# Edge stream: GpSimd waits in the middle of each chunk's gathers for TensorE's last pair of picks

## What is computed

```python
h = (x_flat @ W_gat).reshape(M, HEADS, NUM_EXPERTS)        # M = 16384
src = jnp.concatenate([edge_index[0], loops])              # 262144 edges + 16384 loops
dst = jnp.concatenate([edge_index[1], loops])
e = jax.nn.leaky_relu(a_src[src] + a_dst[dst], negative_slope=0.2)
ee = jnp.exp(e - jax.ops.segment_max(e, dst, num_segments=M)[dst])
denom = jax.ops.segment_sum(ee, dst, num_segments=M)
msg = h[src] * (ee / (denom[dst] + 1e-16))[:, :, None]
agg = jax.ops.segment_sum(msg, dst, num_segments=M)
```

## Time and profile before

| what | value |
|---|---|
| median of 3 runs | 5086.44 us (5078.35 to 5090.78) |
| span of the profiled execution | 5093.1 us |
| span less the runs' median | 6.7 us |
| mean granted clock of TensorE | 0.738 of full speed |
| busy: TensorE, VectorE, ScalarE, GpSimd | 60%, 55%, 46%, 44% of the span |
| gathers of the edge stream | 1632, from 830.4 to 4504.1 us |
| picks of the edge stream | 13056 matmuls |
| turns of VectorE in it (line 1049) | 68, the first at 917.2, the last at 4540.3 us |

### The profile page before, as it was taken

How to read it: one execution, slowest core, us unless ns; L and a number is a source line. 1 busy time by engine, 2 the same in 40 slices (tenths; PEclk the granted TensorE clock), 3 DMA queues, 4 the chain that set the end, 5 groups by cost and what they waited for, 6 DMA issues and landing times. The chain is left out here.

```text
span 5093.1 us, 63233 instructions
## 1 busy us (share of the span) xinstructions
PE 3045.9 (60%) x21149; PEld 2318.6 (46%) x21149; DVE 2806.7 (55%) x5784; ACT 2362.3 (46%) x4288; POOL 2224.4 (44%) x2218
## 2 busy tenths in 40 slices
PE   3656663666566566566566566566566566544775
PEld 2445542554454454455455455455455455432443
DVE  8857883445445445445445445445445445467986
ACT  3636655444444444444444444444434434404886
POOL 7865613334434434434434434434434434426530
PEclk7657775777777777777777777777777777766887
DMA  1111101111111111111111111111111111112101
GB/s 58 24 22 20 22 7 44 24 23 27 31 23 27 31 23 27 31 23 27 31 23 27 31 23 27 31 23 27 31 23 27 31 23 27 25 27 75 38 19 33
DMA packets 157528, 145.13 MB, mean 28 GB/s; under 512 B 71240, under 2 KB 133080, under 8 KB 156776
## 3 DMA queue, kind: packets, MB, share of 16 engines
q1 hardware_dynamic: 88656, 109.49, 6.4%
q0 software_dynamic: 68768, 34.45, 6.2%
HBM read 92.97 MB, written 50.82 MB: 28 GB/s over the span
## 5 line engine op out<-in xcount | busy, mean ns | idle before, releaser
L937 PE MATMUL es_pgot<-hash_space,es_pick 128*128 128x256 bf16 x13056 | 1835.9, 288 | 1423.7 <-issue 1418.8
L857 POOL DMA_INDIRECT es_got<-node_table,late x1632 | 1548.1, 949 | 2127.0 <-DVEq L1077 1649.7
L937 PEld LDWEIGHTS es_pgot<-hash_space,es_pick 128*128 128x128 bf16 x13056 | 1302.8, 101 | 1899.6 <-issue 1742.7
L1019 DVE TENSOR_TENSOR es_prod<-es_pgot,es_own 128x512 f32<-128x512 f32 x272 | 187.7, 690 | 1801.6 <-PE es_pgot L937 1627.7
L871 ACT ACTIVATE es_pick<-es_away,consts 128x512 bf16<-128x512 f32 x1088 | 680.0, 711 | 7.0 <-DMA es_away<-sorted_keys 6.6
L293 POOL DMA_INDIRECT fr_ring<-in_emb,fr_rows x384 | 456.0, 1188 | 209.8 <-issue 112.8
L875 ACT ACTIVATE es_pick<-es_pick,consts 128x4096 bf16<-128x4096 bf16 x136 | 503.6, 3703 | 0.9
L894 ACT ACTIVATE ex_hid<-ex_phid,weights 128x256 f32<-128x256 f32 x128 | 53.6, 470 | 692.7 <-PE ex_phid L944 692.3
L1039 DVE TENSOR_TENSOR es_hot<-es_iota,late 128x1024 bf16<-128x1024 f32 x272 | 331.7, 1219 | 33.4 <-DVE es_st L1079 25.7
L1040 DVE TENSOR_TENSOR es_hot<-es_iota,late 128x1024 bf16<-128x1024 f32 x272 | 330.2, 1214 | 0.0
L894 ACT ACT_TABLE_LOAD x32 | 41.1, 1283 | 559.2 <-PE ex_phid L944 559.2
(11 more groups left out here) (351 smaller groups left out, 4294.6 us busy)
## 6 DMA issues: line engine op xcount, KB each, us to landing
es_away<-sorted_keys SPq DMA_DIRECT2D x68, 512.0 KB
es_got<-node_table,late POOLq DMA_INDIRECT x1632
edge_states<-es_st SPq DMA_DIRECT2D x68, 384.0 KB
expert_outputs<-ex_y SPq DMA_DIRECT2D x64, 256.0 KB
bk_y<-expert_outputs SPq DMA_DIRECT2D x8, 2048.0 KB
fr_ring<-in_emb,fr_rows POOLq DMA_INDIRECT x384
out_dram<-h SPq DMA_DIRECT2D x4, 1024.0 KB, 5.1
late<-in_edges SPq DMA_DIRECT2D x1, 2048.0 KB, 9.3
```

Source lines behind the costliest of these rows:

```text
L857: pool.indirect_dma_start(out=got[:, r, k, :], out_offset=None, in_=table_dram, in_offset=bass.IndirectOffsetOnAxis(ap=src[:, n, k:k + 1]. ...
L937: mm = pe.matmul(p_got[:, q, c * 256:c * 256 + 256], pick[:, r, q // 2, k, at * P:at * P + P], parts[:, part, k], start=(k == 0 and part = ...
```

## The change

One wait is added to GpSimd's program. In every chunk n but the first, after 12 of its 24 gathers, GpSimd waits until `s_got_p` has reached 4n, which is when TensorE has finished pair 3 of chunk n-1. It then issues the other 12.

```diff
                 if n >= 2:
                     pool.wait_ge(s_free[r], n // 2)
                 for k in range(GC):
+                    if n and k == GC // 2:
+                        pool.wait_ge(s_got_p, n * PAIRS)
                     pool.indirect_dma_start(out=got[:, r, k, :], out_offset=None, in_=table_dram,
```

## The result

The changed kernel takes 4844.46 us (median of 4 runs, 4831 to 4854) against 5088.33 us of the kernel before: a ratio of 0.9524, 95% interval 0.9503 to 0.9545. It is faster, as forecast, but by 244 us and not by 136, outside the forecast range (4860 to 5180).

The account below looks back on a forecast made before the run. VectorE waits for TensorE, which crawls while gathers are issued. Turns of 52.5 us, not 54.6, give -134, the stage's start -14, the end +10: -138 on 5093.1, 4955, stated as 4950 us; range 4860 to 5180.

Parts of the forecast that it names:

- The lag of 6.0 us in both bursts: TensorE runs 6.0 us at full rate after each burst of gathers starts, on a stock of ready work, then crawls.
- B: Moved burst of twelve gathers behind pair 3, starting at T-3.6; its crawl lasts T+2.4 to T+15.15, 12.75 us.
- The slower rival: Stock still empty when B starts, so its crawl starts 1.6 us in: 56.7 us a turn, about 5216 us; chance 0.19.
- the stock lasts longer: Rival: 7.5 us of lag in both bursts, crawls 1.5 us shorter each, turn 49.7, 4770 us; chance 0.12.
- A: Burst of twelve gathers that stays, after the buffer is freed: starts T+25.1, crawls from T+31.0 to T+43.85.
- T: Start of one turn of the edge-stream loop; times such as T+20.9 count microseconds from it.
- The stage's start: GpSimd stops after 36 gathers, not 48, so the crawl under the four first pairs ends sooner: -14 us.
- The end: Last three turns: A and B join to one burst of 24; 42, 51 and 46 us against 128.9: +10 us.
- Only the number of gathers counts: No-change rival: crawls sum to what they were, turns within 0.2 us of 54.6, 5070 to 5100 us; chance 0.11.
- Theory A: Experiments: the crawl comes whenever gathers go on over 6 us, however spaced; one fill ahead of each gives ratio 1.055.
- Theory B: Experiments: each gather takes about 1.4 us of a service TensorE needs; gathers 1.44 us apart give ratio 0.79 to 0.90.
- B2: Experiments: the service goes by the gather as such, so half-row gathers crawl as before, ratio 0.96 to 1.02.

Follow-up runs that it names:

- e9: Changed kernel with its wait ahead of the first of the 24 gathers, not the thirteenth; with the crawl 0.9967 of the kernel before, 54.6 us a turn.
- e8: Changed kernel with portions of 8 gathers and two waits instead of one; with the crawl 0.9380 of the kernel before, 50.1 us a turn.
- e15: Changed kernel, unedited, run again against the kernel before, without the crawl: 3396.13 us, ratio 0.9999.
- e7: Kernel before with one GpSimd fill of a scratch tile ahead of every gather, no wait in the middle; with the crawl 4293.67 us, ratio 0.8456.
- e17: Kernel before with one scratch fill ahead of each gather and the wait in the middle; with the crawl 4202.80 us, ratio 0.8230.
- e18: Kernel before with gathers of 64 rows instead of 128 from the third chunk on; with the crawl ratio 1.0179.
- e10: Kernel before with every gather of the edge stream reading the same 128 table rows; with the crawl ratio 0.9995.
- e16: Kernel before with gathers of 64 rows instead of 128 from the third chunk on; without the crawl ratio 0.983.

## Why the forecast was wrong, point by point

*What bounds the kernel: right, in the sets with the crawl.* VectorE waited for TensorE and TensorE for something that goes with the gathers.

*The lag of 6.0 us in both bursts: right as a number, open as a mechanism.* It is 5.8 us (median of the bursts of 12) in the changed kernel, also in B, which starts about 5.3 us after a crawl's end (1484.77 to 1490.08). The slower rival (0.19) fails here: its crawl would have started 1.6 us into B. Whether a stock of ready work is what lasts 5.8 us was only argued. Signals of TensorE that are late while it still runs at full rate fit a rival as well: something behind TensorE fills up and does not hold it until it is full. No run separates the two. At the stage's start fourteen gathers and not twelve had been issued when the first picks began (830.35 to 846.58), which fits either.

*The length of a crawl: wrong, and this is the step that failed.* The prediction took over "the full rate returns 5.0 us after the last gather" from bursts of 24 and charged 12.75 us to a burst of 12. The tail is not a constant, it is the backlog of the burst, 3.2 us after 12: the crawls were 11.4 and 11.0 us. The kernel before had the two lengths that show it: 5.0 us after 24 gathers and 8.2 us after the 48 at the stage's start, 889.00 to 897.20; only the first was used. The measured 4844 us lies in the range of the rival "the stock lasts longer" (4740 to 4890), and its crawls, 1.5 us shorter than forecast, came true; but they were shorter at their end, with a lag of 5.8 and not 7.5 us, so its number fits by luck. A constant tail also makes the second way of the sum (52.7 us) too high, and I raised 52.2 to 52.5 for its sake.

*What a crawl lets through: too much for B, and the clock too cheap.* 19 matmuls in a crawl held for A (19) and not for B: its 12 in 11.35 us are fewer than the 15 in 11.0 us of the earlier trace rows, which the prediction had named as a sign against it. And the 47 matmuls behind B took 7.67 us at a granted clock of 0.66, where 5.7 us for 43 were charged. So the 1.3 us by which B's crawl ended sooner (T+13.9, not T+15.15) were given back: pair 1 was done at T+21.5 against a forecast of T+20.9, A began at T+25.8 and not T+25.1. VectorE's new waiting in the first half came as foretold: 10.5 us in two waits, 4.68 us for pair 0 and 5.80 for pair 1. The first of them is a late signal, which the prediction did not have: by its sum the last matmuls of pair 0 are the first thing done in the crawl. In the second half VectorE waits 9.31 and 3.18 us, 12.5 where some 15 were forecast.

*The sum of a turn: order of events right, size off.* The gain is 3.5 us a turn where 2.1 were forecast: 51.1 us and not 52.5. Over 64 turns that is 89 us of the 106 by which the forecast missed the median. Not all of the 1.4 us is the crawls. Medians over the turns put the take of the last pair at T+47.8, where 48.6 was forecast. The two crawls together are about 3 us shorter than charged, but a later start of A's crawl (0.5 us), fewer matmuls inside B's and slower ones behind both leave only some 0.5 us of it. Another 0.35 us is the step from pair 3's last matmul to the take, charged at 0.5 and measured at 0.15 (so it stood in the earlier trace rows too, 1568.84 to 1568.99). About 0.2 us is the step from the take to the next turn, which is 3.2 and 3.6 us by turns and not always 3.6, and 0.3 us is the raise to 52.5. That the wrong tail did not make the error larger is luck: the clock charged too low stood against it. The turn shown is one of the longest, 51.7 us with pair 3's end at T+48.0 (forecast T+48.1).

*The stage's start: right,* 16.0 us for 14. *The end: wrong sign,* 5.5 us gained for 10 lost; the three turns took 44.0, 43.4 and 36.0 us against 42, 51 and 46. The crawl of the joined burst was charged like a full one under the last two turns. I did not follow those turns in the trace.

*"Only the number of gathers counts" (0.11): refuted* by e9 and e8: 24 gathers a turn in bursts of 24, of 12, and of 8 and 16 give 54.6, 51.1 and 50.1 us.

*The rule that a DMA never contends with a compute engine* (the Trainium skill, "SBUF — State Buffer", "Who interferes with whom"): in three of seven sets nothing here speaks against it, and in the one of them in which the changed kernel ran (e15) its time was the same. In the other four it did not hold. The profile of the kernel before that the prediction used was of the second kind, and nothing in it says that there is a first.

*Theory A of the experiments* (any gathers longer than the stock make a crawl) fell with e7: 1.44 us apart, 0.846 and not 1.055. Theory B, that each gather takes some 1.40 us of a service that TensorE needs too, stands: e7, e17, e18 and the tails. The train of the first stage, 149 gathers in 217 us, fits it: 1.46 us apart on average. By B2 it goes by the gather, not by its rows (e18) or their places (e10). What the service is stays open. It is not the gathers' data: the DMA engines move 0 GB/s between 1564.50 and the crawl's end at 1567.40. And next to no instructions are read from memory meanwhile (12 packets in 3300 us). TensorE's signals are late together with its issue, so it may be their path; no run tests that.

## What to carry to other kernels

A stall that a burst leaves behind can be a backlog: read its tail at two lengths of burst before charging it, since a tail that grows with the count means that requests come faster than they are served, and then spacing them by little more than the missing time is worth far more than moving them (here 0.19 us a gather: 15%, the wait in the middle: 5%, both: 18%). Splitting a burst pays when the slowed engine stands the first microseconds of each part unharmed; moving it whole paid nothing here. Where an engine waits for one that is slowed, compare the signal's arrival with the end of the work it stands for: here 12 us lay between. Measure the kernel before on more than one occasion: a change that is worth 5% in one may be worth nothing in another, and a cure like the fills costs 10% there.

## What the runs showed of the hardware

The same program on the same kind of chip takes 3397 us or 5090 to 5120 us, and stays at one of them for a whole set of runs (up to 16 runs of the kernel before in a set, all within 0.6%). It is not the chip: e15 and e16 ran without the crawl and e17 and e18 with it, on the same chip, some time apart. That leaves what is decided when a program is loaded or when a set is set up; no run here tells which. The traces differ ahead of the edge stream too, though less: its first gather comes at 761 to 770 us without the crawl and at 811 to 833 us with it. Every run of the changed kernel and of the experiments is on record with a span and a granted clock, and the profiled execution of the changed kernel is one of the four timed (4831.48 us, span 4829.7). So "timed without a profile" does not hold for them, and whether there is a crawl when nothing is recorded is not shown.

In a deep crawl TensorE's matmuls are issued singly, in steps of about 0.7 us. In the changed kernel at the stage's start, TensorE in order of time:

```profile
851.33 0.37 PE L939 MATMUL es_pgot<-hash_space,es_pick 128*128 128x256 bf16 x1 [2.43 <-issue]
854.83 0.37 PE L939 MATMUL es_pgot<-hash_space,es_pick 128*128 128x256 bf16 x1 [3.12 <-issue]
857.63 0.37 PE L939 MATMUL es_pgot<-hash_space,es_pick 128*128 128x256 bf16 x1 [2.43 <-issue]
860.44 0.37 PE L939 MATMUL es_pgot<-hash_space,es_pick 128*128 128x256 bf16 x1 [2.44 <-issue]
861.83 0.37 PE L939 MATMUL es_pgot<-hash_space,es_pick 128*128 128x256 bf16 x1 [1.02 <-issue]
862.54 7.72 PE L939 MATMUL es_pgot<-hash_space,es_pick 128*128 128x256 bf16 x49 [0.34 <-issue]
```

The starts are 3.50, 2.80, 2.81, 1.39 and 0.71 us apart: 5, 4, 4, 2 and 1 times 0.70. The 1.40 us that the tails give for a gather are twice that step. I take it for a hint that gathers and TensorE's issue queue for the same thing in units of 0.7 us; it was not tested.

TensorE's signals can arrive long after the rows of the matmuls that send them have ended (trace's records of the semaphores against the modelled ends, medians over 61 turns): 11.3 us for pair 0 and 12.0 us for pair 2 in the changed kernel, 4.8 us for pair 2 in the kernel before, 28.4 us for pair 0 in e9. Without the crawl (e15) no such signal takes more than 0.02 us.
